# Expert lists from scores that leave the gate matmul in the search's layout, and one block for lists and experts

## The reference, cut to what matters

```python
scores = (jnp.tanh(xf @ gate_w.T) + 1.0) * 0.5       # xf: 4096 tokens x 128; 8 experts
vals, idx = jax.lax.top_k(scores.T, k)               # k = 4096 // 8 = 512 tokens for each expert
y = _layernorm(xf[idx.T.reshape(-1)].reshape(k, n, d), ln_gamma, ln_beta)
h = gelu(jnp.einsum('knd,nfd->knf', y, fc1s) + b1s)  # f = 512
o = (jnp.einsum('knf,ndf->knd', h, fc2s) + b2s) * vals.T[:, :, None]
out = xf.at[flat_idx].add(o.reshape(k * n, d))
```

## Time and profile before

| | us |
|---|---|
| median of 3 executions (lowest to highest) | 1027.47 (1027.14 to 1028.28) |
| the profiled execution's own time | 1018.8 |
| its span, from the first to the last instruction | 1016.7 |
| VectorE, TensorE, GpSimd, ScalarE busy | 705.3, 731.2, 521.5, 432.2 |
| mean granted TensorE clock | 0.754 of full speed |

### The profile page before, as it was taken

One profiled execution on the slowest core, in us unless ns is written; L12 is line 12 of the kernel. 1 busy time (PEld: TensorE's weight loads), 2 busy tenths in 40 slices (PEclk: granted clock), 3 DMA queues, 4 the chain that ended last, 5 costly groups with the idle time before them and its releaser, 6 DMA issues. The chain is left out here.

```text
span 1016.7 us, 10897 instructions
## 1 busy us (share of the span) xinstructions
PE 731.2 (72%) x3551; PEld 478.0 (47%) x3551; DVE 705.3 (69%) x1321; ACT 432.2 (43%) x609; POOL 521.5 (51%) x412
## 2 busy tenths in 40 slices
PE   4779978899788997887977663689711870189770
PEld 2355545645456454564655332656611720166550
DVE  7699989999898999999997778422103596812220
ACT  1556935469355595543541554033101273013220
POOL 4057656566575665756665310178760040037864
PEclk9968975799757999578565775589765975559895
DMA  4234433334343343333431533023333006013332
GB/s 126 86 105 144 145 126 137 132 117 151 109 144 126 125 145 128 143 126 129 150 134 63 187 93 88 12 47 43 40 29 91 2 0 181 1 26 46 43 37 21
DMA packets 60067, 96.03 MB, mean 94 GB/s; under 512 B 6392, under 2 KB 40224, under 8 KB 60000
## 3 DMA queue, kind: packets, MB, share of 16 engines
q1 hardware_dynamic: 48192, 85.67, 25.8%
q0 software_dynamic: 11264, 8.66, 6.5%
q10 hardware_dynamic: 560, 1.05, 0.4%
HBM read 81.99 MB, written 13.37 MB: 94 GB/s over the span
## 5 line engine op out<-in xcount | busy, mean ns | idle before, releaser
L280 POOL TENSOR_TENSOR product<-state,c_all 128x1024 f32<-128x1024 f32 x128 | 302.8, 2366 | 218.5 <-DVE state L484 200.4
L613 PE MATMUL m_psum<-ident,product 128*128 128x128 f32 x1024 | 181.2, 334 | 3.7 <-POOL product L280 3.7
L613 PEld LDWEIGHTS m_psum<-ident,product 128*128 128x128 f32 x1024 | 144.7, 172 | 65.0 <-issue 48.4
L470 DVE TENSOR_TENSOR m_psum<-m_psum,dtu 128x1024 f32<-128x1024 f32 x128 | 155.0, 1211 | 20.8 <-PE m_psum L628 20.7
L366 ACT ACTIVATE decay<-dt,decay_rate 128x1024 f32<-128x1024 f32 x128 | 144.3, 1146 | 49.4 <-DVE state L484 45.7
L484 DVE TENSOR_TENSOR_SCAN state<-decay,carry,m_psum 128x1024 f32<-128x1024 f32 x64 | 150.1, 2345 | 4.4
L628 PE MATMUL m_psum<-b_split,pick_r 64*128 64x512 f32 x256 | 116.6, 543 | 48.1 <-DVE state L484 47.6
L484 DVE TENSOR_TENSOR_SCAN state<-decay,m_psum 128x1024 f32<-128x1024 f32 x64 | 146.2, 2285 | 4.4
L703 POOL DMA_INDIRECT f_got<-f_table,f_tokens x64 | 61.8, 966 | 148.9 <-DVE f_tokens L1069 121.4
L628 PEld LDWEIGHTS m_psum<-b_split,pick_r 64*128 64x128 f32 x256 | 47.7, 232 | 111.4 <-DVE state L484 86.5
L1236 ACT ACTIVATE f_hidden<-f_psum,shared_b_T 128x512 f32<-128x512 f32 x64 | 44.0, 688 | 108.7 <-PE f_psum L1274 108.7
(11 more groups left out here) (182 smaller groups left out, 980.1 us busy)
## 6 DMA issues: line engine op xcount, KB each, us to landing
c_all<-c_dram SPq DMA_DIRECT2D x128, 512.0 KB, 3.6
f_table<-f_rows SPq DMA_DIRECT2D x2, 2176.0 KB, 10.3
X<-in_L_attn_a_x SPq DMA_DIRECT2D x4, 512.0 KB, 7.4
f_w_raw<-in_L_ffn_fc2s SPq DMA_DIRECT2D x1, 2048.0 KB, 15.5
between<-f_f SPq DMA_DIRECT2D x1, 2048.0 KB, 8.8
X<-between SPq DMA_DIRECT2D x4, 512.0 KB, 6.9
out<-f_f SPq DMA_DIRECT2D x1, 2048.0 KB, 8.9
f_got<-f_table,f_tokens POOLq DMA_INDIRECT x64, 2.5
```

Source lines behind the costliest of these rows:

```text
L280: pool.tensor_tensor(product[:, n % RING, :], state[:, n % RING, :], c_all[:, n % RING, :], ALU.mult).then_inc(product_ready, 1)
L470: dve.tensor_tensor(pair(n), pair(n), dtu[:, k, :].rearrange("p (a t) -> p a t", t=BANK), ALU.mult).then_inc(drive_ready, 1)
L613: last = pe.matmul(psum[:, Y + i // BT, i % BT * P:(i % BT + 1) * P], product[:, n % RING, i * P:(i + 1) * P], ident[:], start=False, stop ...
```

## The change

The scores come out of the gate matmul as the search wants them. The gate's 8 columns are laid into a zeroed tensor `gate_pad` of 128 x 143, 16 columns apart. A view of 128 columns that starts at J - 1 - j has the gate of expert e in column 16 e + j and zeros elsewhere, so a matmul with span j of `f_T` adds the scores of span j into the partitions 16 e + j and adds zeros into the others. Sixteen such matmuls of 256 columns are summed in one PSUM bank. Then one tanh of 128 x 256 writes `search` and one instruction of VectorE rounds it. The transfers through DRAM and the tensor `score` are gone. The rows' weights come from two transposes of `search` (`turn_scores`) and two instructions of VectorE (`take_weights`), which stand behind the first step of the search. In the first MoE two weight turns stand ahead of the search's steps and one behind them.

The experts' instructions move to the end of the first block's lists, so the barrier between lists and experts is gone; `hidden` and `o` now lie in `f_T` and `f`. GpSimd issues the gathers of experts 0 to 3 at once, and the 16 gathers of experts 4 to 7 in portions of 4, 3, 3, 3, 3 ahead of the scatters of experts 1 to 5; before, they went 4 at a time ahead of the scatters of experts 1 to 4.

```diff
-                sp.wait_ge(score_ready, NB)
-                sp.dma_start(score_dram, score[:]).then_inc(score_stored, 16)
-                sp.wait_ge(score_stored, 16)
-                sp.dma_start(search[:], score_dram.rearrange("e (j t) -> (e j) t", j=J)
-                             ).then_inc(search_loaded, 16)
...
-                sp.wait_ge(weights_ready, 1)
+                sp.wait_ge(weights_ready, HALVES)
...
+                if first_use:
+                    pool.memset(gate_pad[:], 0.0).then_inc(pad_zero, 1)
...
+                for e in range(1, AHEAD):
+                    gather(pool, e)
+                pool.sem_inc(o_free, AHEAD)
+                later = [(e, t) for e in range(AHEAD, E) for t in range(KT)]
+                SHARE = (0, 4, 3, 3, 3, 3, 0, 0)
+                assert sum(SHARE) == len(later)
+                for e in range(E):
+                    first = sum(SHARE[:e])
+                    for other, t in later[first:first + SHARE[e]]:
+                        gather_rows(pool, other, t)
+                    pool.wait_ge(o_ready, e + 1)
...
-                def tanh(g):
-                    act.wait_ge(gated, g + 1)
-                    act.activation(score[:, g * BANK:(g + 1) * BANK],
-                                   psum[0:E, SCORES + g % SCORE_BANKS, :], ACT.Tanh).then_inc(tanh_done, 1)
+                def tanh():
+                    act.wait_ge(gated, 1)
+                    act.activation(search[:], psum[:, SCORES, 0:SPAN], ACT.Tanh).then_inc(tanh_done, 1)
...
                 for g in range(2, NB):
                     take_turned(g)
-                    tanh(g - 2)
-                tanh(NB - 2)
-                tanh(NB - 1)
+                tanh()
...
+                def round_score():
+                    dve.wait_ge(tanh_done, 1)
+                    dve.tensor_scalar(search[:], search[:], 1.0, -1.0, ALU.add,
+                                      ALU.add).then_inc(score_ready, 1)
+
+                def take_weights():
+
+                    dve.wait_ge(score_turned, 1)
+                    for h in range(HALVES):
+                        dve.tensor_scalar(
+                            rows[:].rearrange("p (j h) c -> p h j c", h=HALVES)[:, h, :, DM:ROW],
+                            psum[:, SMALL, h * P:(h + 1) * P].rearrange("p (e j) -> p j e", j=J),
+                            1.0, 0.5, ALU.add, ALU.mult).then_inc(weights_ready, 1)
...
-                        dve.tensor_copy(gate_T[:], psum[:, SMALL, 0:E]).then_inc(small_ready, 1)
+                        dve.wait_ge(pad_zero, 1)
+                        dve.tensor_copy(gate_pad[:, J - 1:J - 1 + P:J], psum[:, SMALL, 0:E]).then_inc(small_ready, 1)
...
-                for g in range(NB):
-                    round_score(g)
-                dve.wait_ge(score_turned, TILES)
-
-                dve.tensor_scalar(rows[:, :, DM:ROW],
-                                  psum[:, SMALL, 0:TILES * E].rearrange("p (i e) -> p i e", e=E), 1.0, 0.5,
-                                  ALU.add, ALU.mult).then_inc(weights_ready, 1)
...
-                dve.wait_ge(search_loaded, 16)
+                round_score()
+                dve.wait_ge(score_ready, 1)
...
                 quarter(0)
+                take_weights()
...
-                        if g > SCORE_BANKS:
-                            pe.wait_ge(tanh_done, g - SCORE_BANKS)
-                        pe.matmul(psum[0:E, SCORES + (g - 1) % SCORE_BANKS, :], gate_T[:],
-                                  f_T[:, (g - 1) * BANK:g * BANK], start=True, stop=True).then_inc(gated, 1)
+                        for j in range((g - 1) * BANK // SPAN, g * BANK // SPAN):
+                            last = pe.matmul(psum[:, SCORES, 0:SPAN], gate_pad[:, J - 1 - j:J - 1 - j + P],
+                                             f_T[:, j * SPAN:(j + 1) * SPAN],
+                                             start=(j == 0), stop=(j == J - 1))
+                        if g == NB:
+                            last.then_inc(gated, 1)
+                pe.wait_ge(cast, 3)
+
+                def turn_scores():
+                    pe.wait_ge(score_ready, 1)
+                    for h in range(HALVES):
+                        last = pe.transpose(psum[:, SMALL, h * P:(h + 1) * P], search[:, h * P:(h + 1) * P],
+                                            ident[:])
                     last.then_inc(score_turned, 1)
...
-                    for n in range(2 * E - STEPS):
+                    for n in range(2):
                         turn_weights(n)
+                    turn_scores()
                     for i in range(STEPS):
                         total(i)
-                        turn_weights(2 * E - STEPS + i)
+                        turn_weights(i + 2)
+                    turn_weights(STEPS + 2)
                 else:
+                    turn_scores()
...
-        with nc.cleanup_on_exit(), ExitStack() as ctx:
...
-            psum = ctx.enter_context(nc.psum_tensor(f"{name}_psum3", [P, 8, BANK], F32))
```

More of the change, by code:

```diff
@@ L690, in moe @@
     table = dram("table", [T, ROW])
-    score_dram = dram("score_dram", [E, T])
-    gamma, b1_T, b2_all, gate_T, w1_T, w2_T = (
-        shared[key] for key in ("gamma", "b1_T", "b2_all", "gate_T", "w1_T", "w2_T"))
+    gamma, b1_T, b2_all, gate_pad, w1_T, w2_T = (
+        shared[key] for key in ("gamma", "b1_T", "b2_all", "gate_pad", "w1_T", "w2_T"))
     with nc.cleanup_on_exit(), ExitStack() as keep:
@@ L783, in moe @@
             gated = sem("gated")
+            pad_zero = sem("pad_zero")
             tanh_done = sem("tanh_done")
@@ L1072, in _, with scale_rows @@
                 dve.wait_ge(tokens_ready, GROUPS * P // LO)
+                def scale_rows(e, r):
+                    dve.wait_ge(y_turned, e + 1)
+                    dve.tensor_scalar(y_T[:, r, :], psum[:, YT + r, :], gamma[:, 0:1], gamma[:, 1:2],
+                                      ALU.mult, ALU.add).then_inc(y_ready, 1)
+                scale_rows(0, 0)
+                with dve.Fori(0, E // AHEAD) as m:
+                    for n in range(AHEAD):
+                        r = n % 2
+                        scale_rows(AHEAD * m + n + 1, 1 - r)
+                        dve.wait_ge(o_summed, AHEAD * m + n + 1)
+                        dve.wait_ge(o_free, AHEAD * m + n + 1)
+                        dve.wait_ge(gathered[n], 16 * KT * (m + 1))
+                        dve.tensor_tensor(
+                            o[:, n],
+                            psum[:, OUT + r, :].rearrange("p (t d) -> p t d", d=DM),
+                            b2_all[:, bass.ds(AHEAD * m + n, 1), :].broadcast_to([P, KT, DM]),
+                            ALU.add).then_inc(o_biased, 1)
+                        dve.wait_ge(o_biased, AHEAD * m + n + 1)
+                        for t in range(KT):
+                            last = dve.tensor_scalar(o[:, n, t, :], o[:, n, t, :],
+                                                     got[:, n, t, bass.ds(DM + AHEAD * m + n, 1)], None,
+                                                     ALU.mult)
+                        last.then_inc(o_ready, 1)
             @block.tensor
```

132 lines of the change are left out of this document (39 added, 93 removed).

## The result

The changed kernel took **1024.17 us** (median of 7 runs, 1023.33 to 1026.54), the kernel before 1027.73 in the same comparison (7 runs, 1027.14 to 1029.15): ratio 0.9966, 95% interval 0.9954 to 0.9977. It is faster by 3.6 us, where 22.0 were forecast; 1024.17 lies far above the range, which ended at 1011.0. The profiled execution took 1023.96 with a span of 1022.2. That is longer than the profiled execution of the kernel before (1018.8, span 1016.7), which the sum had started from; what became of that difference is part of the answer.

What follows compares the result with a forecast made beforehand. Each MoE was taken as bound by one chain across engines, so savings count twice. Terms 7.6 - 0.5 + 1.95 + 1.95 = 11.0 us per MoE, 22.0 off the 1027.5 median, gave 1005.5 us, range 1001.0 to 1011.0.

Steps and rivals of the forecast that it cites:

- the slower rival: Sixteen gathers in one queue: expert 0's rows land only with the last, 15.5 us later; 1036.5 us, chance 0.02.
- the wait for 2.4: Before each MoE's first scatter, GpSimd, done early with 16 gathers, would stand idle for 2.4 us.
- Score path: End of each MoE's front: without score transfers and most tanh and roundings, search starts 7.6 us earlier, bounds 6.3 to 8.3.
- the rival of 2.6 us: ScalarE's table load stands behind the gate wait, tanh 1.28 later per MoE, 2.6 in all: 1008.1 us, chance 0.09.
- Weights of the scores: Two strided VectorE pieces after the first search step: a loss of 0.5 us per MoE, between 0.4 and 0.85.
- Table write: Table written on SyncE before the first gather: costs nothing, with about 12 us of cover.
- One block: Lists to experts without a barrier: TensorE starts transposes at once, gain 1.95 us per MoE, bounds 1.0 to 4.4.
- Spread: Gathers in portions 4,3,3,3,3 leave two bare waits before the last scatters, not three: gain 1.95 us per MoE, bounds 0.9 to 2.35.
- The sum: All terms together: 7.6 - 0.5 + 1.95 + 1.95 = 11.0 us for a MoE, 22.0 for both.
- The clock: TensorE's clock stays at 1.2 GHz for experts 4 to 7, expert 7 comes 7.4 late: 1020 us, chance 0.03.
- the rival of late rows: Experts 6 and 7 are late by 2 us, so the spread gives nothing: 1009.3 us, chance 0.10.
- one of the signs named for being wrong: In the experts' part, scatters 6 and 7 waiting for VectorE would show the prediction wrong.

Runs made afterwards that it cites:

- experiment 1: The kernel before, unchanged, timed and profiled once more: 1027.37 us, ratio 1.0002.
- the fresh profile: The second profile of the unchanged kernel before, taken with its rerun: span 1028.6 us, 11.9 more than its first profile.
- experiment 5: The changed kernel, with GpSimd waiting for the landing of an expert's four gathers before issuing the next four (experts 1 to 3): 997.42 us, ratio 0.9707.
- experiment 12: The changed kernel with landing waits after rows of four, but gathers of experts 4 to 7 four ahead of each of scatters 1 to 4: 1000.27 us.
- (8): The changed kernel with gathers of experts 1 to 3 held back, plus twelve plain SyncE loads of 128 rows beside the lists: 1008.53 us, ratio 0.9817.
- (4): The kernel before, with only its gathers of experts 1 to 3 moved ahead of the barrier, sixteen in a row: 1048.86 us, ratio 1.0209.
- (11): The changed kernel in rows of four gathers, each pause a GpSimd memset of 128x1500 instead of a landing wait: 994.76 us, ratio 0.9672.
- experiment 3: The changed kernel, with GpSimd waiting for expert 0's scaled rows before issuing the gathers of experts 1 to 3: 1006.05 us, ratio 0.9788.

## Why the prediction was wrong, step by step

**The step that failed** is the argument against the slower rival: "twelve gathers in a row already landed 2.5 us each after issue". The sixteen landed as fast. What a long row delays is TensorE's issuing and its counts, and with them the wait for 2.4 that GpSimd was to have ahead of the first scatter became 17.90 and 19.08. The rival's price was right to a tenth, for another reason than it gave: counted from the first gather, expert 0's rows are scaled at 23.65 in the changed kernel (663.22 - 639.57) and at 8.12 with rows of four (649.57 - 641.45), 15.5 later, beyond the 11 us from which it was said to decide. Both accounts tie expert 0 to the end of the row, one by its landing, the other by the counts that come 2.9 after it, so that the figures meet is in part luck. I had asked only whether the *rows* come late, and gave the rival 0.02. The row of the kernel before that I leaned on came from an execution in which its twelve gathers disturbed nothing; experiment 1 shows that this was not its usual state.

The rest of the rival came with it: it said a loss of 4.5 us for each MoE, and the last scatters end 4.5 and 4.8 later than in the profile of before.

**The second failed step** is the sentence "nothing in the MoE stages is known to differ, so I take the 22.0 off there too". The 8.7 us between the profiled execution and the median were mostly the same stall: the kernel before pays about 5 us in each MoE too, and for that reason the change does not lose against the median. Against the fresh profile the last scatters end only 0.1 and 0.8 earlier in the two MoEs; what makes up the rest of the 3.6 us is not shown.

**Score path**, forecast 7.6, bounds 6.3 to 8.3: measured 8.27 and 8.25, against the fresh profile 8.41 and 8.37, just over the bound that was to refute it. The mechanisms are as told: one L1017 of 2.47, and the table load not behind the wait for the gates (it started 1.2 before they ended, so the rival of 2.6 us had nothing to collect). The 0.6 of difference lies ahead of the last gates. The sum let the last four transposes start when VectorE had made all of their tiles. In the trace the first of them is at 832.11 and the others follow the tiles, and the gates start at 833.49, where the sum has 834.1 in this trace's clock. The Trainium skill (ScalarE: Activation LUTs, section "What ACT_TABLE_LOAD costs") has 2.66 for a switch; the trace shows 1.28 again.

**Weights of the scores**, forecast a loss of 0.5: two pieces in 0.48. Between search start and first gather 0.26 and 0.64 of the gain were lost.

**Table write**: issued at 616.81 and landed 9.5 us later; the first gather is at 639.57, so 13 us of cover are left, against the 12 of the forecast.

**One block**, forecast 1.95: TensorE does go from lists to transposes without a pause (experiment 5, 648.34), and joining the blocks is what lets the row of 16 form. In experiment 5 first gather to first scatter take 24.70, in the profile of before 24.53: what the joining gives goes into the pauses (4.4 us in all), and the term comes to about 0.

**Spread**, forecast 1.95: 2.1 and 1.8 by experiment 12, with two bare waits as told.

**The sum**, once the row is broken: the end of the last scatter is 9.9 and 9.6 us earlier than in the profiled execution of before, where 11.0 was forecast: score path and spread held, one block gave nothing. That the whole takes 997.42, where the sum from that execution said 996.8, is in part luck, for some 2 us of it come from a first MoE that starts earlier (563.6 in place of 565.7). The condition that all terms rest on, other engines undisturbed by the row, did not hold.

**The clock** was no part of it: in the window from 639.50 it was granted 0.50, as in the earlier trace rows. Of the rival of late rows one scatter of four shows something, 1.2 us; that it waited for VectorE was one of the signs named for being wrong.

Open is by what path a row of gathers holds up TensorE, and why one execution of the kernel before escaped. One rival was not tried and is not excluded. That execution's trace has every landing update of the gathers, and all the others lack nearly half of them or more. The loss of updates could come with the stall, or the recording of so many updates could be what holds TensorE's counts back. Rows of four speak against a simple tie, since 273 to 288 of 512 updates are there and the counts of the lists are still at most 0.7 late. The record gives a span and a clock of the core for every timed execution too, so the times don't tell whether an execution without recording has the stall. What the runs exclude: the rows' landing, DMA being busy (0.20), traffic of the same size from another queue (8), the joined block (4), and GpSimd's being busy as such (11). Whether another engine's counts would be held up as TensorE's are, was not tried; the one of ScalarE in experiment 3 that was on time came before TensorE's were late.

The Trainium skill (DMA: Bandwidth & Descriptors, section "Anatomy of one DMA — SWDGE (gpsimd) path") says of descriptor generation that many descriptors can be emitted before its cost shows. For the DMAs themselves the trace of the changed kernel agrees (landings at 2.1 to 2.7 in the row of sixteen); for the engine beside them the runs show a small cost after four gathers and a growing one with each further gather.

## What to carry to other kernels

Don't let GpSimd issue a long unbroken row of indirect transfers beside or just ahead of work that other engines must be told of: break it after four, with a wait that is needed anyway or a piece of other work. When a step moves DMA issues together, price the row as a whole and ask not only when its data land but whether the other engines' instructions and counts get through. And when a profiled execution is 0.9% shorter than the median, take a second profile before building a sum on it; here most of the difference was the very mechanism that decided. Look also whether the two traces are equally complete. Whether the advice holds for executions that nothing records is open, as said above.

## What the hardware showed that was not expected

- TensorE's list matmuls get their first unexplained hole 4.8 to 6.0 us after the first gather's issue, whatever the length of the row (4.4 and 4.7 beside the plain loads); in four of the MoEs with rows of four there is none. With rows of four the holes make up at most 0.9. In longer rows they go on, and a new group of matmuls comes only every 0.7 or 1.4 us. The last list matmul starts, after the first gather and over both MoEs: 6.6 to 7.5 with rows of four (6.6 and 6.7 without a hole), 8.5 and 8.7 with five, 9.0 and 9.6 with six, 10.2 and 11.9 with eight, 10.7 and 16.3 with sixteen in the changed kernel, 8.8 and 17.7 in experiment 4.
- TensorE's counts were registered 11.9 and 8.9 us late in a row of sixteen (first MoE), 6.0 and 5.6 late in a row of twelve (experiment 3), in both cases at a time 2.2 to 2.9 after the row's last issue had ended; with rows of four the counts of the lists are 0.01 late in experiments 5 and 12, and 0.3 and 0.7 in 11.
- The size by row length (changed kernel, median): 16: 1024.17; 4 and 12: 1006.05; 8, 4, 4: 1006.64; 6, 6, 4: 999.73; 5, 5, 6: 1001.19; 4, 4, 4, 4: 997.42 and 994.76. These versions differ in where their pauses stand as well as in the length of the rows.
